# Two PSUM banks for turned probabilities, one bank for four side threads, in the second layer of a decoder

## The reference

```
x = LN(x + attn(x))          # 16 heads of 16, causal softmax, + gated memory term, output product
x = LN(x + xattn(x, ctx))    # each token attends to 64 indexed ctx tokens (indices repeat)
x = LN(x + ffn(x))           # 8 experts of rank 64, two branches, running sums, router softmax

def attn: softmax(q k^T * scale, causal) v
def xattn: kv = (ctx @ W_down)[indices] @ W_up;  softmax(q k^T * scale) v;  @ W_out
```

## Time and profile before

| | |
|---|---|
| median of 3 runs | 2637.9 us |
| profiled execution, its time | 2646.27 us |
| its span | 2644.5 us |
| TensorE busy | 2243.5 us, 85% of the span |
| VectorE busy | 1341.9 us, 51% |
| ScalarE busy | 998.1 us, 38% |
| mean granted TensorE clock | 0.876 of full speed |

### The profile page before, as it was taken

The page is one execution under the profiler, slowest core; times in us unless marked ns, Lnnn a source line. Parts: engine busy times, 40 slices in busy tenths (PEclk is TensorE's granted clock), DMA queues, the critical chain, the costliest instruction groups (busy, mean ns, idle before and its releaser), DMA issues. The chain is left out here.

```text
span 2644.5 us, 38948 instructions
## 1 busy us (share of the span) xinstructions
PE 2243.5 (85%) x13569; PEld 1574.3 (60%) x13637; DVE 1341.9 (51%) x3927; ACT 998.1 (38%) x3145; POOL 363.0 (14%) x639
## 2 busy tenths in 40 slices
PE   8688898898889988896818588899999999999887
PEld 4356566666677755575704355566666666666655
DVE  7245455564645454322129466665656656566331
ACT  3133535343545443352202135453444444444220
POOL 2044141423232324001000000000000000000000
PEclk9768868877899998897958699998999999999888
DMA  8000000000232210344651000000000000000000
GB/s 296 9 4 1 5 5 9 9 5 9 94 104 83 80 31 29 114 162 172 231 135 48 14 10 1 10 5 5 10 5 10 5 10 5 6 5 5 5 1 9
DMA packets 50763, 116.27 MB, mean 44 GB/s; under 512 B 8192, under 2 KB 30464, under 8 KB 46976
## 3 DMA queue, kind: packets, MB, share of 16 engines
q1 hardware_dynamic: 49024, 109.49, 12.3%
q0 software_dynamic: 1536, 4.20, 0.5%
HBM read 90.20 MB, written 23.46 MB: 43 GB/s over the span
## 5 line engine op out<-in xcount | busy, mean ns | idle before, releaser
L690 ACT ACTIVATE PRS<-PT 128x384 f32<-128x384 f32 (+1 forms) x512 | 265.6, 519 | 847.0 <-PE PT L621 846.4
L753 DVE TENSOR_REDUCE negmax<-SM 128x2 f32<-128x512 f32 x432 | 283.9, 687 | 229.1 <-PE SM L584 121.8
L621 PE MATMUL PT<-const_sb,PRS 128*128 128x128 f32 x1664 | 314.2, 307 | 40.0 <-ACT PRS L690 33.9
L705 ACT ACTIVATE PRS<-SM,negmax 128x128 f32<-128x128 f32 x608 | 248.3, 423 | 142.6 <-DVE negmax L753 142.6
L621 PEld LDWEIGHTS PT<-const_sb,PRS 128*128 128x128 f32 x1664 | 210.1, 155 | 134.9 <-issue 101.4
L2756 DVE TENSOR_SCALAR arena<-arena 128x256 bf16<-128x256 bf16 x1024 | 210.5, 281 | 9.2 <-PE SC L2774 8.2
L574 PE MATMUL SM<-haloU,QM 32*128 32x128 f32 (+1 forms) x1056 | 182.2, 388 | 12.0 <-ACT PRS L705 9.5
L574 PEld LDWEIGHTS SM<-haloU,QM 32*128 32x128 f32 x1056 | 136.5, 223 | 27.3 <-ACT PRS L705 13.0
L574 PE MATMUL SC<-haloU,QM 32*128 32x128 f32 (+1 forms) x480 | 120.0, 408 | 34.6 <-ACT PRS L705 34.6
L2774 PE MATMUL SC<-arena,identb 128*128 128x256 bf16 x1024 | 139.1, 279 | 2.7 <-DVE arena L2756 2.7
L636 PE MATMUL OA<-PRS,big 128*32 128x256 f32 (+1 forms) x1024 | 136.5, 393 | 3.0 <-ACT PRS L690 3.0
(11 more groups left out here) (565 smaller groups left out, 4109.9 us busy)
## 6 DMA issues: line engine op xcount, KB each, us to landing
arena<-lay SPq DMA_DIRECT2D x50, 1024.0 KB, 4.9
arena<-lay SPq DMA_DIRECT2D x1, 7700.5 KB, 21.2
rows<-OT SPq DMA_DIRECT2D x2, 3456.0 KB, 31.9
arena<-lay SPq DMA_DIRECT2D x1, 3862.0 KB, 19.9
arena<-rows SPq DMA_DIRECT2D x25, 128.0 KB, 2.8
arena<-lay SPq DMA_DIRECT2D x25, 128.0 KB, 5.3
rows<-arena SPq DMA_DIRECT2D x25, 128.0 KB, 4.6
rows<-OT SPq DMA_DIRECT2D x1, 2432.0 KB, 21.3
```

The costliest lines, as they stand in the source:

```text
L621: ins = pe.transpose(bank[:, o:o + P], PR[n % 4][:, t, k * P:(k + 1) * P], ident)
L690: act.activation(dst, src, ACT.Copy).then_inc(S("probs_moved"), 1)
L705: ins = act.activation(dst, src, ACT.Exp, bias=negmax[:, h, r:r + 1], accum_out=rsum[:, t, h:h + 1])
L753: st.post(dve.tensor_reduce(negmax[:, ORDER[s], :], two(banks[s % NB]), AX.X, ALU.max, negate=True), S("max_ready"))
```

## The change

The tally and the count get both PT banks for their flips. The side bank "a" goes away, and what used it (start, end, one product of feed) now claims bank "j", PJ[0], together with middle and ask. No instruction is added or taken away, apart from waits on semaphores. Since `len(hs.flips)` is now 2, the order inside a slot changes too: on TensorE the values follow both flips instead of standing between them, and on ScalarE (`early` is now false) the slot runs exponentials, move, exponentials, move instead of move, move, exponentials, exponentials.

```diff
-        TALLY = Heads(QM, VS, YT[:], rinv, S("asked_t"), [PT[0]])
-        COUNT = Heads(QM_count, VS_count, ZT[:], rinv_c, S("asked_k"), [PT[0]])
+        TALLY = Heads(QM, VS, YT[:], rinv, S("asked_t"), PT)
+        COUNT = Heads(QM_count, VS_count, ZT[:], rinv_c, S("asked_k"), PT)
...
-            for name, bank in (("a", PT[1]), ("j", PJ[0]), ("f", PJ[1])):
+            for name, bank in (("j", PJ[0]), ("f", PJ[1])):
...
-                ba, bj, bf = (Bank(*spots[name]) for name in ("a", "j", "f"))
+                bj, bf = (Bank(*spots[name]) for name in ("j", "f"))
+                ba = bj
```

## The result

The changed kernel takes 2686.26 us (median of 4 runs, 2682.47 to 2688.04) against 2637.14 for the kernel before (now four runs), a ratio of 1.0176 with a 95% interval of 1.0145 to 1.0207: 49 us slower. The direction was forecast; the size (2659, at most 2682) was not.

What follows compares the result with a forecast made beforehand. TensorE was taken to set the pace, busy 125.06 of each period's 132.8 us. Losses 37.7, gains 21.4 and clock 5.5 gave +21.8 us, hence 2659 on the median's scale, with a range of 2632 to 2682.

Steps and rivals of the forecast that it cites:

- the clock's term: Layer 1: stalls bring one more 1.2 GHz stretch in each of five periods, 8.5 us, less 3 given back: +5.5 us.
- the bound of 31 us: Upper bound on clock loss: 1.7 us for each of 18 new stalls over 1 us or near it.
- Rival 3: The clock follows the stalls: two more slow stretches in each of six periods, 20 us, giving 2675; chance 0.15.
- Loss 1: Count: start's claims of the joint bank wait behind middle's, 1.43, 0.85 and 0.53 us in three slots; 16.3 us in all.
- Loss 2: Tally slot 2: end waits behind ask, 1.26 us five times and 2.0 first, 8.3 in all; earlier exponentials credited nothing.
- Loss 3: Tally after end's layernorm: first move between late exponentials adds 0.35 to a scores wait of 0.82, six times, 2.1 us.
- Loss 4: Threads without an attention share one bank: 8.5 us in the opening, 2.5 us at ask of batch 7.
- Gain 1: Tallies and counts: scores wait less because exponentials start sooner; 21.4 us in all, 5.7 of it in the last count.
- the 136 to 138 of the text: Sign of being right: a period of tally and count goes from 132.8 us to 136 to 138.
- a period over 139 with a clock under 0.93: One sign of being wrong: a tally with its count takes over 139 us at a granted clock under 0.93.
- Rival 1: The gains win: later waits absorb most collisions, whose price falls from 38 to 13 us, leaving 2630; chance 0.12.
- Rival 2: No change: about half the losses are absorbed or the counts' gains bring more; 2638, from 2627 to 2650; chance 0.26.

Runs made afterwards that it cites:

- old_order: The changed kernel with the earlier order of values, moves and exponentials put back on TensorE and ScalarE; 2717.53 us, 1.0294 of the kernel before.
- order_one: The kernel before with only ScalarE's slot reordered to first move, both exponentials, second move; 2628.38 us, 0.9945 of the kernel before.
- join_only: The changed kernel with flips back on one PT bank in the old order, PJ[0] still shared; 2714.52 us, 1.0295 of the kernel before.
- tally_two: The kernel before with two flip banks for the tally only, end and feed's one product moved to PJ[0]; 2666.21 us, ratio 1.0071.
- apart_join: join_only with each slot's side threads dealt in another order, putting other matmuls between claims of PJ[0]; 2642.67 us, 0.9998 of the kernel before.
- join_fill: join_only plus 120 unread matmuls (the fillings) into PT[1], ahead of four claims expected to stall; 2688.17 us, 1.0192 of the kernel before.

## Why the prediction was wrong

**The step that failed is the size of the clock's term.** The prediction put it as "I take one more such stretch in each of five periods, 8.5 us, and give back 3", +5.5 us. The block measured 42.1 us more busy time for the same matmuls. Even the bound of 31 us was too low, since it priced each stretch at the 1.7 us seen behind the earlier trace rows. Rival 3 named the mechanism with a chance of 0.15 and 20 us. Two things were missed: more stretches at 1.2 GHz came, and they are not of fixed length. Counted in the clock records of the two traces, the block has 37 such stretches after the change, 258 us in all, against 21 and 158 us before: 16 more where the prediction took five, and a loss of 2.6 us for each (42.1 by 16) instead of 1.7. Nor is the loss even. Of the 42.1 us, 9.1 fall in the opening, 12.0 in the last tally with its count, and 13.4 in the four full periods ahead of that, 1.1 in the least and 6.3 in the most. The last tally with its count, before and after:

```profile
2332.40:2454.80 122.40, 115.14 (x731) 80.16 (x733) 78.58 (x283) 52.53 (x151) 2.07 (x3) 0.96 0.02 5
...
2362.90:2496.10 133.20, 127.16 (x731) 87.08 (x734) 78.69 (x283) 50.98 (x151) 2.07 (x3) 0.86 0.02 5
```

The windows of the last tally in the kernel after:

```profile
2363.00:2376.00 13.00, 10.47 (x64) 7.30 (x63) 8.33 (x23) 6.69 (x28) 0.00 (x0) 0.87 0.08 21
2376.00:2398.00 22.00, 21.16 (x88) 12.72 (x87) 7.78 (x23) 6.74 (x25) 0.00 (x0) 0.61 0.00 1
2398.00:2406.00 8.00, 7.45 (x52) 4.90 (x51) 6.02 (x21) 1.55 (x8) 0.69 (x1) 1.00 0.00 0
2406.00:2424.00 18.00, 16.52 (x70) 10.65 (x71) 8.90 (x25) 6.02 (x26) 0.00 (x0) 0.53 0.00 1
2424.00:2440.00 16.00, 16.00 (x88) 12.37 (x88) 5.73 (x25) 4.34 (x9) 0.69 (x1) 1.00 0.04 14
```

The grant falls around a wait (2.53 us ahead of scores, then 0.84 ahead of L1449) and stays at 1.2 GHz for most of 22 us, through two slots of scores, flips and values, and again for 18 us behind the wait of 1.15. At half speed, some 17 us in each is 8 us of loss, five times the price used.

**Loss 1 was right.** 1.36, 1.74 (the 0.78 flip wait and 0.85 were forecast, 1.63) and 0.78 us, against 1.43, 1.63 and 0.86. **Loss 2** was half too large in a full period, 1.26 for 0.84, but right for the first (1.9 for 2.0). The clause "I take no more than nothing" from the earlier exponentials was the slip: ScalarE, done with its exponentials and moves, begins the queries' copies 0.04 us behind the last of their matmuls, and not 0.28 as before. **Loss 3** was right: 1.15 for 0.82 + 0.35. **Loss 4** was right in idle time: in the opening TensorE idled 8.9 us more (8.5 forecast), but it was also busy 9.1 us more, at 1.2 GHz, and so the stretch grew by 18 us.

**Gain 1** was right in mechanism and nearly in size. Its cause, exponentials behind a second move, is shown by old_order and order_one. The last count gave less than its 5.7: from ask of batch 7 to the end TensorE idled 1.7 us less, with loss 4's 2.5 inside. All terms of idle time together were forecast at +16.3 us and measured at +13.2. The period shown came to 140.1 us (the four full ones, 137.1 to 142.0), past the 136 to 138 of the text, with an idle time of 10.4 (7.7 + 3.2 by the terms) and the rest clock. The sign of being wrong, "a period over 139 with a clock under 0.93", was met in its first half only: the clock was 0.94 in it.

**Rival 1** (later waits absorb the stalls) fell: the stalls stand in full in every period. **Rival 2** fell with it. The two rules of the Trainium skill fared unequally. The Trainium skill (TensorE: Matmul & The Clock Gate, "A second HAM failure mode: psum-queue depth-cycling") says that small idle times between groups of matmuls make the clock swing; the trace agrees (mean grant 0.93 to 0.89, and back to 0.93 with the fillings). The Trainium skill (Perfetto Trace Analysis, "Matmuls") advises to rotate groups through PSUM banks; that holds for the side threads (join_only, 2.95% slower), and for the flips it took the waits away and no run shows that time was gained by it (old_order against join_only).

Left open: how long a stall, and where, brings the clock down. Busy time differs between kernels with the same idle time (tally_two and apart_join, 1074 and 1051 us at 118 idle), and these runs only show that filling or moving the waits recovers it. Nor does every stretch at 1.2 GHz stand behind a wait. In the period shown, the flips at 2191.41 took 1.88 us for the 1.04 of the slot before, though the 24 us ahead of them hold no wait over 0.16:

```profile
2183.48 1.04 PE L621 MATMUL PT<-const_sb,PRS 128*128 128x128 f32 x8
...
2191.41 1.88 PE L621 MATMUL PT<-const_sb,PRS 128*128 128x128 f32 x8
```

## What to carry to other kernels

When TensorE is the bound, price a new wait twice: its length, and a stretch at 1.2 GHz behind it, which in the tallies and counts here lasted up to 17 us; then read busy time for the same count of matmuls before and after, and look first whether the records are complete. When an edit brings an order along with a resource, test the order alone: here it was the whole gain and needed no bank. Give a new dealing its own control. And deal the threads that share a bank, or that wait for the same engine, so that another thread's matmuls stand between their steps.

## What the runs showed of the hardware

TensorE, at work for 21.16 of 22 us, was at 1.2 GHz for most of them, after a wait of 0.84 us (windows above). It was at full speed again behind the residual product and during the output product (L1465 at 2395.78 took 1.33 us where the one at 2107.53 took 1.12; L396 behind it took 1.89 both times) in the one case, and behind the count's value products (L2680), where the experts' products (L2828) begin, in the other. And 120 matmuls whose result nobody reads made a kernel 26 us faster (join_fill against join_only).
